# Query rows of 27 sequences loaded in 32-number runs and turned by VectorE in 32 by 32 blocks, in place of TensorE transposes

## The reference, cut to what matters

```
bias = braak_embed[itok][..., None]           # (32, 256): one number per sequence and row
q    = x + bias                               # row s of sequence b gets embed[itok[b], s]
attn = softmax(q @ side^T)                    # 256 x 256 for each sequence
o    = attn @ side
out  = x + moe_ffn(rmsnorm(o) * norm_w)       # 8 experts of rank 16 over a base FFN of 1024, top 2
```

## Time and profile before

| | us |
|---|---|
| median of three runs (1307.0 to 1309.33) | 1308.72 |
| the profiled execution | 1308.66 |
| its span, from first to last instruction | 1306.9 |
| TensorE busy | 1301.1 |
| VectorE busy | 843.5 |
| ScalarE busy | 527.5 |
| GpSimd busy | 249.9 |

### The profile page before, as it was taken

One profiled execution on the slowest core, in us unless ns is written; L12 is line 12 of the kernel. 1 busy time (PEld: TensorE's weight loads), 2 busy tenths in 40 slices (PEclk: granted clock), 3 DMA queues, 4 the chain that ended last, 5 costly groups with the idle time before them and its releaser, 6 DMA issues.

```text
span 1306.9 us, 18607 instructions
## 1 busy us (share of the span) xinstructions
PE 1301.1 (100%) x7286; PEld 1139.3 (87%) x7286; DVE 843.5 (65%) x1558; ACT 527.5 (40%) x991; POOL 249.9 (19%) x213
## 2 busy tenths in 40 slices
PE   9999999999999999999999999999999999999998
PEld 8999998888888888888888888888888888888887
DVE  6776656756665576656675667557675666565556
ACT  6776753333343344333333334333333343243332
POOL 3556540202011020202020202011020202020200
PEclk9999999999999999999999999999999999999999
DMA  9555810020202020201102020202020101102000
GB/s 294 145 147 154 233 43 33 2 73 2 73 2 73 1 73 1 59 16 33 42 2 73 1 73 2 73 1 74 2 73 1 57 17 35 40 1 73 1 17 17
DMA packets 71791, 69.56 MB, mean 53 GB/s; under 512 B 7050, under 2 KB 62744, under 8 KB 71576
## 3 DMA queue, kind: packets, MB, share of 16 engines
q1 hardware_dynamic: 71392, 68.37, 17.5%
q10 hardware_dynamic: 312, 0.02, 0.0%
HBM read 51.27 MB, written 17.10 MB: 52 GB/s over the span
## 4 chain that ended last, share of the span: by engine, by line
PE 98%; ACT 1%; DVE 0%; issue 0%; DVEq 0%
PE bank L1205 31%; PE bank L1204 31%; PE bank L1206 30%; PE bank L1330 2%; PE bank L1257 2%; PE bank L1308 1%; PE bank L1250 1%; ACT prob L663 0%; PE bank L1216 0%; ACT qT_hi L646 0%; ACT kT_hi L647 0%; DVE probT_lo L886 0%; DVE x_out L1148 0%; PE bank L1295 0%; ACT value_hi L657 0%
## 5 line engine op out<-in xcount | busy, mean ns | idle before, releaser
L1076 DVE TENSOR_TENSOR act_a<-silu_a,bank 128x512 f32<-128x512 f32 x128 | 87.7, 686 | 210.9 <-PE bank L1206 194.2
L754 ACT ACTIVATE br_hi<-act_br 128x512 fp32r<-128x512 f32 x128 | 81.0, 633 | 188.6 <-DVE act_br L1087 188.6
L747 ACT ACTIVATE silu_b<-bank 128x512 f32<-128x512 f32 x128 | 76.3, 596 | 187.9 <-PE bank L1206 187.0
L590 POOL TENSOR_TENSOR t_lo<-t_in,t_hi 128x512 fp32r<-128x512 f32 x32 | 40.6, 1291 | 552.2 <-ACT t_hi L734 552.2
L1205 PE MATMUL bank<-w2T_lo,s_hi 128*128 128x256 f32 x512 | 144.7, 283 | 0.0
L1206 PE MATMUL bank<-w2T_hi,s_lo 128*128 128x256 f32 x512 | 143.3, 280 | 0.0
L1204 PE MATMUL bank<-w2T_hi,s_hi 128*128 128x256 f32 x512 | 142.7, 279 | 0.0
L1084 DVE TENSOR_TENSOR act_b<-silu_b,bank 128x512 f32<-128x512 f32 x128 | 88.0, 688 | 81.4 <-PE bank L1206 80.4
L743 ACT ACTIVATE silu_a<-bank 128x512 f32<-128x512 f32 x128 | 75.8, 592 | 134.1 <-PE bank L1206 134.0
L609 POOL TENSOR_TENSOR v_lo<-v_full,v_hi 128x512 fp32r<-128x512 f32 x64 | 94.5, 1508 | 136.6 <-ACT v_hi L739 136.6
L1097 DVE TENSOR_TENSOR br_lo<-act_br,br_hi 128x512 fp32r<-128x512 f32 x128 | 104.7, 818 | 5.6 <-ACT br_hi L754 3.1
(11 more groups left out here) (197 smaller groups left out, 3242.2 us busy)
## 6 DMA issues: line engine op xcount, KB each, us to landing
kv<-in_fside_BxSxS SPq DMA_DIRECT2D x32, 256.0 KB, 3.3
x_in<-in_x SPq DMA_DIRECT2D x32, 256.0 KB, 4.0
t_scratch<-oT SPq DMA_DIRECT2D x32, 256.0 KB, 2.5
t_in<-t_scratch SPq DMA_DIRECT2D x16, 512.0 KB
x_out<-in_x SPq DMA_DIRECT2D x16, 512.0 KB, 4.0
out<-x_out SPq DMA_DIRECT2D x30, 256.0 KB, 4.0
rho<-scale_scratch SPq DMA_DIRECT2D x16, 256.0 KB
rstd<-scale_scratch SPq DMA_DIRECT2D x16, 256.0 KB
```

The source lines that it names most:

```text
L747: nc.scalar.activation(silu_b[:, :], h1_bank[j % 2][:, :], ACT.Silu).then_inc(silu_b_ready, 1)
L754: nc.scalar.activation(br_hi[j % 2][:, :], act_br[j % 2][:, :], ACT.Copy).then_inc(br_hi_ready, 1)
L1076: nc.vector.tensor_tensor(act_a[j % 2][:, :], silu_a[j % 2][:, :], h3_bank[j % 2][:, :], ALU.mult).then_inc(act_a_ready, 1)
```

## The change

Sequences 0 to 4 stay as they were. From sequence 5 on:

- x is loaded by four DMAs, one for each group g of 32 columns (the group of the same number in both halves), in runs of 32 numbers (128 bytes). Row `8 b + j` of x goes to partition `32 g + b`, where g is the group of columns, at a place given by j and the half.
- GpSimd adds the bias in this layout, in one 128x512 addition in place, with a table `bias_rep` that holds the bias by (partition, j, sequence).
- VectorE turns each 32 by 32 block (`turn_q`), so that the columns lie on partitions. It does so two steps ahead, between `keep_gate` and `probT_low`.
- ScalarE and VectorE make the high and low parts of q out of this SBUF tensor instead of PSUM, with outputs that step over 8 numbers (`in_blocks`), which puts the rows into their order. The high part of q has its own wait; that of k waits for TensorE's transposes as before.
- TensorE makes only the four transposes of the side rows. Once, in step 0, it makes eight small products for `bias_rep`, from an embedding table that GpSimd has spread; ScalarE copies the result.

The diff, cut to its core:

```diff
+BLK = 32
+BLOCKS = S // BLK
+FIRST_TURNED = 5
...
+        def as_blocks(ap):
+            return ap.rearrange("p h d -> p (h d)")
+        def blocks_of(ap):
+            return as_blocks(ap).rearrange("p (j c b) -> p j c b", c=DC, j=BLOCKS)
+        def in_blocks(ap):
+            return ap.rearrange("p (c b j) -> p j c b", c=DC, j=BLOCKS)
...
+            x_blocks = x.rearrange("b (s j) (c g a) -> b g s (j c) a", s=BLK, c=DC, a=BLK)
             def load_xs(c):
                 if c >= RING:
                     sp.wait_ge(q_ready, c - RING + 1)
+                if c >= FIRST_TURNED:
+                    if c - RING >= FIRST_TURNED:
+                        sp.wait_ge(q_turned, turned_no(c - RING))
+                    for g in range(P // BLK):
+                        sp.dma_start(x_in[c % RING][g * BLK:(g + 1) * BLK].rearrange("p h (n a) -> p (h n) a", a=BLK),
+                                     x_blocks[c, g]).then_inc(xs_loaded[c % RING], 16)
+                    return
...
+            def spread_embed():
+                pool.wait_ge(embed_loaded, 16)
+                nc.gpsimd.tensor_copy(embed_rep[:, :, :].rearrange("k j (g b) -> k j g b", b=BLK),
+                                      embed_in[:, :].rearrange("k (b j) -> k j b", j=BLOCKS).unsqueeze(2).to_broadcast(
+                                          [STAGES, BLOCKS, P // BLK, BLK])).then_inc(embed_spread, 1)
+            def add_block_bias(c):
+                pool.wait_ge(bias_rep_copied, 1)
+                pool.wait_ge(xs_loaded[c % RING], xs_count(c))
+                blocks = as_blocks(x_in[c % RING][:, :, :]).rearrange("p (j n) -> p j n", j=BLOCKS)
+                rows = bias_rep[:, :, c].unsqueeze(2).to_broadcast([P, BLOCKS, DC * BLK])
+                nc.gpsimd.tensor_tensor(blocks, blocks, rows, ALU.add).then_inc(q_ready, 1)
...
             def qk_high(c):
-                act.wait_ge(qkT_ready, c + 1)
-                nc.scalar.activation(qT[c % 2][0][:, :], qT_bank[:, :], ACT.Copy).then_inc(qT_hi_ready, 1)
+                if c >= FIRST_TURNED:
+                    act.wait_ge(q_turned, turned_no(c))
+                    nc.scalar.activation(in_blocks(qT[c % 2][0][:, :]), blocks_of(q[c % 2][:, :, :]), ACT.Copy
+                                         ).then_inc(qT_hi_ready, 1)
+                    act.wait_ge(qkT_ready, c + 1)
+                else:
+                    act.wait_ge(qkT_ready, c + 1)
+                    nc.scalar.activation(qT[c % 2][0][:, :], qT_bank[:, :], ACT.Copy).then_inc(qT_hi_ready, 1)
...
             def copy_gate():
                 act.wait_ge(gate_wT_ready, 1)
+                act.wait_ge(bias_rep_ready, 1)
...
+            def copy_bias_rep():
+                nc.scalar.activation(bias_rep[:, :, :].rearrange("p j b -> p (j b)"), o_bank[:, S:S + BLOCKS * BATCH],
+                                     ACT.Copy).then_inc(bias_rep_copied, 1)
...
+            def turn_q(c):
+                dve.wait_ge(q_ready, c + 1)
+                dve.wait_ge(qkT_ready, c - 1)
+                nc.vector.transpose(as_blocks(q[c % 2][:, :, :]), as_blocks(x_in[c % RING][:, :, :])
+                                    ).then_inc(q_turned, 1)
             def qk_low(c):
                 dve.wait_ge(qT_hi_ready, c + 1)
+                hi, lo = qT[c % 2]
+                if c >= FIRST_TURNED:
+                    nc.vector.tensor_tensor(in_blocks(lo[:, :]), blocks_of(q[c % 2][:, :, :]), f32(in_blocks(hi[:, :])),
+                                            ALU.subtract)
...
             # VectorE's step, behind keep_gate and ahead of probT_low
+                if FIRST_TURNED <= c + 2 < BATCH:
+                    turn_q(c + 2)
...
             def transpose_qk(c):
-                pe.wait_ge(q_ready, c + 1)
-                transpose_seq(q[c % 2], qT_bank)
+                if c < FIRST_TURNED:
+                    pe.wait_ge(q_ready, c + 1)
+                    transpose_seq(q[c % 2], qT_bank)
...
+            def place_bias():
+                pe.wait_ge(embed_spread, 1)
+                for j in range(BLOCKS):
+                    last = nc.tensor.matmul(o_bank[:, S + j * BATCH:S + (j + 1) * BATCH], embed_rep[:, j], stage_hot[:, :],
+                                            start=True, stop=True)
+                last.then_inc(bias_rep_ready, 1)
...
                 if jobs_here and c == 0:
                     weight_job(jobs_of(c)[1])
                     transpose_gate()
+                    place_bias()
...
                 if c == 1:
                     pe.wait_ge(gate_w_copied, 1)
+                    pe.wait_ge(bias_rep_copied, 1)
```

More of the change, by code:

```diff
@@ L148, in adaln_moe_ffn @@
         gram_diag = sb(early, "gram_diag", [P, SC, P])
+        bias_rep = sb(early, "bias_rep", [P, BLOCKS, BATCH])
+        embed_rep = sb(early, "embed_rep", [STAGES, BLOCKS, P])
         embed_in = sb(early, "embed_in", [STAGES, S])
@@ L207, in adaln_moe_ffn @@
         bias_copied = sem("bias_copied")
+        embed_spread = sem("embed_spread")
+        bias_rep_ready = sem("bias_rep_ready")
+        bias_rep_copied = sem("bias_rep_copied")
         xs_loaded = sems("xs_loaded", RING)
@@ L211, in adaln_moe_ffn @@
         q_ready = sem("q_ready")
+        q_turned = sem("q_turned")
         kT_ready = sem("kT_ready")
@@ L351, in adaln_moe_ffn, with xs_count, turned_no @@
         T0_STEPS = range(27, 29)
+        def xs_count(c):
+            plain = sum(k % RING == c % RING for k in range(min(c + 1, FIRST_TURNED)))
+            turned = sum(k % RING == c % RING for k in range(FIRST_TURNED, c + 1))
+            return 16 * (plain + P // BLK * turned)
+        def turned_no(c):
+            return c - FIRST_TURNED + 1
+        def as_blocks(ap):
[4 more added lines that the diff above has]
+            return ap.rearrange("p (c b j) -> p j c b", c=DC, j=BLOCKS)
         def group_in(c):
@@ L562, in value_low @@
                                         ).then_inc(value_lo_ready, 1)
+            def add_block_bias(c):
[4 more added lines that the diff above has]
+                nc.gpsimd.tensor_tensor(blocks, blocks, rows, ALU.add).then_inc(q_ready, 1)
             def add_bias(c):
+                if c >= FIRST_TURNED:
+                    add_block_bias(c)
+                    return
                 pool.wait_ge(q_ready, c)
                 pool.wait_ge(qkT_ready, c - 1)
-                pool.wait_ge(xs_loaded[c % RING], 16 * (c // RING + 1))
+                pool.wait_ge(xs_loaded[c % RING], xs_count(c))
                 for h in range(SC):
@@ L594, in t_low @@
                 last.then_inc(t_lo_ready, 1)
+            spread_embed()
             for c in range(BATCH):
@@ L714, in step @@
                     weight_high(jobs_of(c)[0])
+                if c == 0:
+                    copy_bias_rep()
                 if jobs_here and len(jobs_of(c)) == 2:
@@ L862, in add_first_bias @@
                 last.then_inc(q_ready, 1)
+            def turn_q(c):
[3 more added lines that the diff above has]
+                                    ).then_inc(q_turned, 1)
             def qk_low(c):
                 dve.wait_ge(qT_hi_ready, c + 1)
-                nc.vector.tensor_tensor(qT[c % 2][1][:, :], qT_bank[:, :], f32(qT[c % 2][0][:, :]), ALU.subtract)
+                hi, lo = qT[c % 2]
+                if c >= FIRST_TURNED:
+                    nc.vector.tensor_tensor(in_blocks(lo[:, :]), blocks_of(q[c % 2][:, :, :]), f32(in_blocks(hi[:, :])),
+                                            ALU.subtract)
+                else:
+                    nc.vector.tensor_tensor(lo[:, :], qT_bank[:, :], f32(hi[:, :]), ALU.subtract)
                 dve.wait_ge(kT_hi_ready, c + 1)
```

## The result

The changed kernel takes 1311.25 us (median of 11 runs, 1309.53 to 1312.64) against 1308.79 us for the kernel before (1307.0 to 1309.33). The ratio is 1.0020, with a 95% interval of 1.0011 to 1.0030: about 2.5 us slower, where 9.4 us faster was forecast. The time is also above the prediction's widest range of 1296.5 to 1310. The profiled execution took 1310.46 us.

A forecast was written before the change was run, and what follows sets the result against it. TensorE, busy 1301.1 of 1306.9 us, was taken as the bound. 1308.66 - 11.75 (transposes) + 1.55 (routing steps) + 0.8 (start) = 1299.3 us; own range 1297 to 1302 (chance 0.63), wide range 1296.5 to 1310.

The forecast's parts named there:

- Removed transposes: TensorE, sequences 5 to 31: four q transposes fewer per step, 0.435 us each time, 11.75 us in all.
- The packets: x transfers: 14 ns per 128-byte packet, so 1.8 us a step against 0.8 for 1 KB packets.
- I cost it at nothing ... the offsets put it where it rarely can.: VectorE's qT_lo waiting for GpSimd's addition: costed at nothing; at worst 0.25 us a step, up to 7 us in all.
- a conflict in 818 against 689 ns: Expert tiles: two alike VectorE forms with two SBUF inputs differ in mean time, read as GpSimd holding something in common.
- the transposes wait if b is over 0.86: Eleven routing steps: probability transposes wait if extra VectorE work b exceeds 0.86 us; with two ScalarE steps, 1.55 us lost.
- will be over-full ... which the lead absorbs: Tile-load steps, DMA share 0.97 of 5.10 us: over-full in a few steps, hidden by loads issued about two steps ahead.
- The transfer of short runs becomes the bound: Rival, chance 0.12: short x packets decide from 23 ns; 1321 us at 30 ns, 1393 at 51 ns.
- x late only in the over-full steps: One form of the rival that the change does less than it says: 1302 to 1306 us, chance 0.08.
- The stride: Strided q copies: ScalarE's qT_hi 0.52 us, bounds 0.49 and 1.05; VectorE's qT_lo 0.69, upper end 1.4; both hidden.
- the two steps that pass through ScalarE: Two routing steps where exponentials already come late because ScalarE waits for VectorE: save nothing, 2 x 0.44 us lost.
- VectorE becomes the bound: Rival, chance 0.17: block transpose and qT_lo together exceed 2.3 us; result 1302 to 1314 us, about 1307.
- The sixteen instructions for bias_rep: TensorE at the start: eight added products, 1.8 us, partly in idle time; 0.8 us lost, bounds 0 and 2.9.

The follow-up runs named there:

- kernel 8: Changed kernel with one more wait, putting GpSimd's block addition behind the step's row maximum: 1309.32 us, 1.0007 of the kernel before.
- kernel 6: Changed kernel with GpSimd's block addition given one tensor input plus a per-partition number (bias wrong for some rows): 1308.91 us, 1.0007 of the kernel before.
- kernel 7: Kernel before, with GpSimd's two one-input bias additions joined into one 128x512 two-input addition: 1311.35 us, 1.0026 of the kernel before.
- kernel 5: Changed kernel with both 1 KB x runs and q parts written in runs of 32 numbers: 1304.54 us, 0.9969 of the kernel before.
- kernel 2: Changed kernel with each x load as one DMA in 1 KB runs: 1305.27 us, 0.9972 of the kernel before.
- kernel 3: Changed kernel with four x DMAs a step kept, each moving 32 partitions in 1 KB runs: 1305.48 us, 0.9977 of the kernel before.
- kernel 4: Changed kernel with the second expert tile's loads issued after steps 28 to 30 instead of 24 to 26: 1307.21 us, 0.9992 of the kernel before.
- kernel 1: Changed kernel with q's two parts written in runs of 32 numbers instead of words 32 bytes apart: 1309.49 us, 1.0009 of the kernel before.
- kernel 9: Changed kernel with GpSimd's addition behind the row maximum and the second tile's loads after steps 28 to 30: 1302.81 us, 0.9961 of the kernel before.

## Why the prediction was wrong, point by point

**Right.** Removed transposes: 0.43 to 0.48 a step measured in steps 4 to 10, 19 and 20, for 0.435. The block transpose: 0.707 mean for 0.69. x issues: 0.64 to 0.66 each where the queue is not full, the upper of the two estimates. The packets: they took 19.5% of 16 x 1308.6 us, 4083 us, and before 17.5% of 16 x 1306.9, 3659 us. The 27 sequences have 27 x 2048 = 55296 short packets for 27 x 256 = 6912 long ones, these at the 51 ns of the mean. So the short ones took (4083 - 3659 + 6912 x 0.051) / 55296 = 14.0 ns, for 14.

**Wrong 1, 3.7 of the 4.6 us: "I cost it at nothing ... the offsets put it where it rarely can."** The step that failed is the term for GpSimd's addition, put at nothing. Moving the addition alone (kernel 8) gives 3.7 us back in the routing steps. The prediction had seen a conflict in 818 against 689 ns, but checked it for qT_lo alone. The short routing instructions have their tensors in SBUF too, and stand where the addition now stands, right behind value_lo. The old addition stood there too, from 78.23 on in the step shown, and cost g_key 0.1 us at most (0.29 for 0.20); it had one input. Kernels 6, 7 and 8 show this from three sides. The Trainium skill (SBUF — State Buffer, Terms) has the pair locked for the full instruction, and the loser blocked: 0.20 us alone against 0.73 to 0.86 beside the two-input addition agrees. The Trainium skill (SBUF — State Buffer, Who interferes with whom) makes no exception for a one-input GpSimd instruction that reads SBUF, when VectorE's has two SBUF inputs; here one of 128x64 took 0.29 to 0.37 us beside such a one and ended long before it, so here the measurement decides.

**Wrong 2, inside the routing steps: "the transposes wait if b is over 0.86".** b is the VectorE work between probT_lo and the row maximum. It was 1.32 in the changed kernel (76.47 to 77.79), 0.91 in kernel 6 and 0.75 in kernel 8, with steps of 5.28, 4.93 and 4.78 us. Each less 4.65 is 0.63, 0.28 and 0.13, which puts the point at 0.69, 0.63 and 0.62, not 0.86. The chain of kernel 5 shows what closes the loop: row maximum, exponentials, value_hi, oT, probT_hi, probT_lo, the routing instruction (from 82.18 to 82.97), the next maximum.

```profile
78.22 0.70 DVE neg_max L952
...
79.31 0.65 ACT prob L716 x3
79.96 0.52 ACT value_hi L710
80.48 0.49 ACT oT L729
80.97 0.50 ACT probT_hi L723
81.47 0.02 issue
81.49 0.69 DVE probT_lo L957
82.18 0.79 DVE g_logits L1007
...
83.51 0.70 DVE neg_max L952
```

From 78.22 to 83.51 are 5.29 us, the length of the step. The prediction let probT_lo start by the ordinary offsets, as if the exponentials' delay did not come back through ScalarE. Its 0.86 is also not quite its own sum: exponentials that end at 3.4 + b and are wanted at 4.29 give 0.89. The two mistakes work on the same instruction, so their prices are not two terms to be added.

**Wrong 3, 6.4 us: "will be over-full ... which the lead absorbs".** The step that failed is the overlap: the lead was taken to hide the extra transfers, and it did not. The over-full steps were seen, the sizes of packet and issue were right, and the conclusion was not worked out. The windows before had a DMA share of 0.97 in such a step, and 1.0 us of DMA time more was added to each. Six steps in a row carry tile loads, and the lead is two. Kernels 2 and 3 lay it on the short packets, 4 on their meeting with the tile loads. Two rivals were near. "The transfer of short runs becomes the bound" asked for dearer packets (30 ns) in every step, and not for the place where transfers were full already; its turning point of 23 ns rests on 1.7 us for side rows and store, where the prediction's own numbers leave 2.8 - 0.8 = 2.0. "x late only in the over-full steps" named the place, but as a case of a few us gained; what TensorE waited for there were the side rows queued behind x, 6.4 us. Of these, long runs give back 4.6 to 5.3; kernel 5 comes to 47.78 for a forecast of 47.2. In kernel 3 at least, what is left includes the wait for GpSimd: its t_in takes 1.36 and 1.29 us, for 0.76 before.

**Mis-sized, and mostly hidden.** The stride: ScalarE's copy lasts 1.20 us. From its start to the next one's are 1.06 (in the changed kernel 76.00 to 77.06), which is the measure of the prediction's 0.52 and is at its upper bound of 1.05. VectorE's qT_lo lasts 1.16 for 0.69, below the upper end of 1.4. The stride costs 0.5 us in step 18, and 0.5 in step 29 (6.42 in kernel 2, 5.94 in kernel 5): the two steps that pass through ScalarE, which the prediction had as saving nothing. Elsewhere these profiles show little of it. The prediction's rival "VectorE becomes the bound" wanted 2.3 us for transpose and qT_lo, and they take 1.87 (1.72 between starts, its own measure). In the routing steps of the changed kernel VectorE has no gap, which looks like that rival; it fell because 0.4 us less on VectorE (kernel 1) changed nothing there: the loop through ScalarE is as long. The Trainium skill (SBUF — State Buffer, Door 1: The DMA port swizzle) was right in direction that words on separate lines cost something; TensorE's transposes, which showed no such cost, did not carry over to the other two engines. The addition took 1.06 where nothing held it, for 1.30.

**The start.** The sixteen instructions for bias_rep took 1.95 us for 1.8. This profile reached its first probability transposes at 14.68 us for 13.65, 1.03 later for 0.8; of that 0.29 were there ahead of them (q transposes at 10.82 for 10.53), which leaves 0.74 for the sixteen. Between profiles of kernels with the same instructions the start moves by more than this. Kernels 1 and 4 were there at 12.93 and 12.91 us. The first transposes of side rows show where that comes from, in the changed kernel and then in kernel 1:

```profile
6.32 1.06 PE L1334 MATMUL bank<-ident,kv 128*128 128x128 f32 x4
```

```profile
5.53 0.60 PE L1334 MATMUL bank<-ident,kv 128*128 128x128 f32 x4
```

TensorE's first microseconds run at about half pace, until 9.4 us in the changed kernel and until 4.7 in kernels 1 and 4. What ends that no row shows, for the granted clock reads 1.00 throughout in these three. Kernels 2, 8 and 9 lost time at another place: from 16.5 to 18.4 us their granted clock was 0.50 (1.2 GHz), where the changed kernel had 1.00 (2.4 GHz), and their step 1 took 6.26 or 6.27 us for 4.64. TensorE had been busy without a gap before it fell.

Of kernel 9's distance to the forecast, 3.5 us, some 0.9 lie in the routing steps, 1.2 in the tile steps, 0.3 in steps 19 and 20, and 1.2 in the start (32.68 us at step 3 for 31.46), where the clock's 1.6 lie.

## What to carry to other kernels

When work moves onto GpSimd, list every VectorE instruction beside it whose tensors all lie in SBUF, the short ones first. A GpSimd instruction with two inputs can hold such a one until it ends (here all but the block transpose), and an exchange of a long one-input instruction for a shorter two-input one can cost time. Put it with an explicit wait where it meets VectorE work that reads PSUM, or where nobody waits for its result yet, as in kernel 8. When a change makes transfers dearer, sum them in the fullest stretch and not in the ordinary step: a share of 0.97 has no room, and what is lost is paid by whichever load stands behind in the queue.

## What the runs showed of the hardware

- A VectorE instruction of 128x64 with two inputs and all tensors in SBUF took 0.20 us alone, 0.29 to 0.37 beside a one-input GpSimd instruction and 0.73 to 0.86 beside a two-input one, and ended within 0.1 us of it. With one input it was held by the two-input addition as well (0.81 us for 0.18), and two single-input instructions of 128x8 also by a one-input addition (0.47 and 0.48 for 0.17). It works both ways: GpSimd's addition, 1.06 us, took 1.87 behind VectorE's qT_lo.
- GpSimd added 128x512 float32 numbers in 1.04 to 1.06 us with two inputs, where one-input additions took 1.57 in one instruction and 1.85 in two.
- Copies of 128x512 in words 32 bytes apart took 1.9 times as long on ScalarE, for read and write alike (1.20 for 0.64), and about 1.6 times as long on VectorE (1.16 for 0.75, or 0.70 in kernel 5).
- VectorE's 32 by 32 block transpose of 128x512 float32 took 0.69 to 0.74 us beside GpSimd's two-input value_lo, and as much where part of it ran with GpSimd idle; no run has the two-input addition beside it.
- In HBM to SBUF transfers, a run of 128 bytes took about 14 ns of a DMA engine, by the working above, and a run of 1 KB about 51, if the mean packet stands for it: for 256 KB that is 1.8 us of all 16 engines against 0.8.
